# Attention over heads: four row groups of scores per batch, one block of values, and reciprocals written wide and turned

## What is computed

```python
x = rmsnorm(layernorm(hidden), norm_w)
q = (x @ wq.T).reshape(B, L, NH, HD)
k = (memory @ wk.T).reshape(B, M, NH, HD)
v = (memory @ wv.T).reshape(B, M, NH, HD)
attn = softmax(where(mask, einsum('blhd,bmhd->bhlm', q, k) * scale, -inf))
out = einsum('bhlm,bmhd->blhd', attn, v).reshape(B, L, C) @ wo.T
x = x + tanh(g) * sigmoid(x @ wg.T) * out
```

## Time and profile before

| | |
|---|---|
| median of 3 runs | 1286.46 us (1286.46 to 1287.14) |
| profiled execution, its span | 1286.6 us |
| PE busy | 1210.8 us |
| DVE busy | 676.6 us |
| ACT busy | 578.8 us |
| first scores to last values of the first attention | 34.9 to 419.6 us |

### The profile page before, as it was taken

One profiled execution on the slowest core, in us unless ns is written; L12 is line 12 of the kernel. 1 busy time (PEld: TensorE's weight loads), 2 busy tenths in 40 slices (PEclk: granted clock), 3 DMA queues, 4 the chain that ended last, 5 costly groups with the idle time before them and its releaser, 6 DMA issues. The chain is left out here.

```text
span 1286.6 us, 25693 instructions
## 1 busy us (share of the span) xinstructions
PE 1210.8 (94%) x7835; PEld 1023.1 (80%) x7836; DVE 676.6 (53%) x1411; ACT 578.8 (45%) x1387; POOL 424.5 (33%) x514
## 2 busy tenths in 40 slices
PE   7998999999999879889999998999999999999995
PEld 7877777787787657667777777889999889999995
DVE  6656545545445989944576554642234552424241
ACT  5554445455356768872111112543344453434341
POOL 1102211211213656400015742244434334443443
PEclk9999999999999999989999999999999999999997
DMA  9100000000000122022000413764445766545454
GB/s 334 39 18 20 18 1 20 18 1 18 18 18 2 34 69 65 29 96 85 1 0 2 160 41 130 221 142 85 78 103 117 201 144 146 137 85 136 86 135 71
DMA packets 54335, 100.36 MB, mean 78 GB/s; under 512 B 5094, under 2 KB 21990, under 8 KB 54262
## 3 DMA queue, kind: packets, MB, share of 16 engines
q0 software_dynamic: 15824, 37.76, 15.5%
q1 hardware_dynamic: 38438, 61.65, 14.7%
HBM read 72.91 MB, written 26.48 MB: 77 GB/s over the span
## 5 line engine op out<-in xcount | busy, mean ns | idle before, releaser
L1925 PE MATMUL t_H<-m_W,t_xT 128*128 128x352 f32 x1632 | 281.9, 328 | 7.3 <-DVE m_W L2003 5.7
L1925 PEld LDWEIGHTS t_H<-m_W,t_xT 128*128 128x128 f32 x1632 | 263.3, 189 | 10.1 <-DVE m_W L2003 8.1
L1893 POOL DMA_INDIRECT out_dram<-t_ys,t_sid x68 | 109.5, 1610 | 225.0 <-ACT t_ys L1954 110.6
L1970 ACT ACTIVATE t_sl<-t_H 128x352 f32<-128x352 f32 x68 | 31.6, 465 | 175.6 <-PE t_H L1925 175.6
L759 ACT ACTIVATE pr<-SC,neg 128x128 f32<-128x128 f32 x256 | 90.1, 377 | 38.2 <-DVE neg L973 38.2
L47 PE MATMUL t_Y<-m_W,t_hT 128*128 128x512 f32 (+1 forms) x207 | 88.1, 426 | 4.9 <-issue 3.0
L2048 DVE TENSOR_TENSOR t_hT<-t_TH,t_hT 128x384 fp32r<-128x384 f32 x68 | 37.8, 556 | 101.8 <-ACT t_hT L1991 100.6
L2024 DVE TENSOR_TENSOR t_h<-t_H,t_sl 128x352 f32<-128x352 f32 x68 | 35.6, 523 | 104.8 <-ACT t_sl L1970 104.8
L1954 ACT ACTIVATE t_ys<-t_Y,t_wcol 128x512 f32<-128x512 f32 x69 | 47.4, 687 | 95.3 <-PE t_Y L49 95.3
L49 PE MATMUL t_Y<-m_W,t_hT 128*128 128x512 f32 (+1 forms) x207 | 82.5, 398 | 0.0
L48 PE MATMUL t_Y<-m_W,t_hT 128*128 128x512 f32 (+1 forms) x207 | 82.2, 397 | 0.0
(11 more groups left out here) (508 smaller groups left out, 3216.8 us busy)
## 6 DMA issues: line engine op xcount, KB each, us to landing
m_raw<-in_L_ffn_w_dram SPq DMA_DIRECT2D x28, 704.0 KB, 5.3
m_raw<-in_L_ffn_w_dram SPq DMA_DIRECT2D x14, 512.0 KB, 6.8
CT<-in_ctx_dram SPq DMA_DIRECT2D x8, 512.0 KB, 3.7
X<-in_x_dram SPq DMA_DIRECT2D x4, 1024.0 KB, 13.4
rows_d<-rows_first SPq DMA_DIRECT2D x16, 256.0 KB, 2.0
out_dram<-X SPq DMA_DIRECT2D x3, 1024.0 KB, 4.3
m_raw<-in_L_ffn_w_dram SPq DMA_DIRECT2D x14, 192.0 KB, 6.7
CT<-in_ctx_dram SPq DMA_DIRECT2D x8, 256.0 KB, 2.7
```

Source lines behind the costliest of these rows:

```text
L1893: pool.indirect_dma_start(out=m["out_rows"][:, :], out_offset=bass.IndirectOffsetOnAxis(ap=sid[:, b:b + 1], axis=0), in_=ys[:, b, :], in_o ...
L1925: x_ = pe.matmul(bk[b % 2][:, 0:I], xT[:, b % 2, jx, k, :], W13[:, jw, k, j, :], start=k == 0 and jx == jw, stop=k == KC - 1 and jx == 1)
```

## The change

- The scores of a whole batch are one step `S`: four mask matmuls and 16 score matmuls, in four row groups and four banks SC, one bank for each row group. `sm` and `pT` now count heads by row group, and `pT` has four buffers.
- The values of a batch are one step `pv` in a bank of M instead of two in O.
- `rc` writes the reciprocals at once over 128x512, each 32 times, into `o`; `bc` turns `o` with four transposes through T, and ACT copies it back to `o`; the product (formerly `on`) is DVE's part of `pv`.
- `gs` has one buffer instead of two, `mrow` two rows instead of four with `mk` one batch ahead.
- The plan of all four groups is written anew: `pv`, `oT` and `oP` of a batch stand behind the next batch's `S`.

The diff, cut; the removed lines of the plan are in the kernel above.

```diff
         mcol = sb("mcol", [P, NB])
-        mrow = sb("mrow", [P, GB, S], BF16)
...
-        gs = sb("gs", [P, 2, D])
+        gs = sb("gs", [P, D])
...
-        pT = sb("pT", [P, 2, HQ, S])
+        pT = sb("pT", [P, HQ, HQ, S])
...
-        T, M, SC = bank("T", 2), bank("M", 2), bank("SC", 2)
-        O, REC = bank("O", 1)[0], bank("REC", 1)[0]
+        T, M, SC = bank("T", 2), bank("M", 2), bank("SC", HQ)
...
                 break
             plan += steps(
-                f"Sa.0 xT.2 Sb.0 sm.0 sm.1 v.0 st.-2 st.-1 cT.2 ra.-1 xT.3 {d[0]} g.0 rb.-1 pT.0 cT.3 q.1.0 rd.-1 Sa.1 pT.1 Sb.1 "
...
+                f"S.0 pv.-1 sm.0 v.0 oT.-1 xT.2 xT.3 sm.1 oP.-1 pT.0 mk.1 {d[0]} g.0 pT.1 sm.2 q.1.0 st.-2 st.-1 cT.2 sm.3 ra.-1 q.1.1 "
+                f"cT.3 rb.-1 {d[1]} pT.2 q.1.2 rd.-1 {d[2]} pT.3 rc.0 q.1.3 u.-2 sf.-4 sf.-3 uT.-2 u.-1 bc.0 fm.-2 "
+                f"S.1 pv.0 sm.4 v.1 oT.0 uT.-1 {d[3]} sm.5 oP.0 pT.4 mk.2 {d[4]} g.1 pT.5 sm.6 fm.-1 k.1.0 sm.7 k.1.1 nm.4 nm.5 pT.6 sf.-2 {d[5]} k.1.2 "
+                f"pT.7 rc.1 k.1.3 xT.4 sf.-1 bc.1 "
+                f"S.2 pv.1 sm.8 v.2 oT.1 xT.5 cT.4 sm.9 oP.1 pT.8 mk.3 {d[6]} g.2 pT.9 sm.10 q.2.0 cT.5 st.0 sm.11 q.2.1 {d[7]} pT.10 q.2.2 "
+                f"nm.6 nm.7 pT.11 rc.2 q.2.3 bc.2 "
+                f"S.3 pv.2 sm.12 v.3 oT.2 {d[8]} sm.13 oP.2 {d[9]} pT.12 st.1 mk.4 ra.0 g.3 pT.13 sm.14 rb.0 k.2.0 sm.15 rd.0 k.2.1 pT.14 u.0 k.2.2 "
+                f"pT.15 rc.3 uT.0 u.1 k.2.3 bc.3 fm.0 uT.1 fm.1 ", g)
         plan += steps(
-            "Sa.0 xT.2 Sb.0 sm.0 sm.1 v.0 st.-2 st.-1 cT.2 ra.-1 xT.3 g.0 rb.-1 pT.0 cT.3 cx.0 cx.1 q.1.0 rd.-1 Sa.1 pT.1 Sb.1 "
...
+            "S.0 pv.-1 sm.0 v.0 oT.-1 xT.2 xT.3 sm.1 oP.-1 pT.0 mk.1 g.0 pT.1 sm.2 q.1.0 st.-2 st.-1 cT.2 sm.3 ra.-1 q.1.1 "
+            "cT.3 cx.0 cx.1 rb.-1 pT.2 q.1.2 rd.-1 pT.3 rc.0 q.1.3 u.-2 sf.-4 sf.-3 uT.-2 u.-1 bc.0 fm.-2 "
+            "S.1 pv.0 sm.4 v.1 oT.0 uT.-1 sm.5 oP.0 pT.4 mk.2 g.1 pT.5 sm.6 fm.-1 k.1.0 sm.7 k.1.1 pT.6 sf.-2 k.1.2 "
+            "pT.7 rc.1 k.1.3 cx.2 cx.3 sf.-1 bc.1 "
+            "S.2 pv.1 sm.8 v.2 oT.1 sm.9 oP.1 pT.8 mk.3 ta.0 tb.0 pT.9 sm.10 g.2 tc.0 sm.11 pT.10 an.0 qh.0 ks.0 st.0 "
+            "pT.11 rc.2 bc.2 "
+            "S.3 pv.2 sm.12 v.3 oT.2 sm.13 oP.2 pT.12 st.1 ra.0 g.3 pT.13 sm.14 rb.0 sm.15 an.1 qh.1 ks.1 pT.14 rd.0 u.0 aS.0.0 "
+            "pT.15 rc.3 aT.0 bc.3 pv.3 oT.3 aS.0.1 ag.0.0 aT.1 aS.0.2 ag.0.1 "
             "oP.3 uT.0 u.1 fm.0 ", NG - 1)
...
-        SPLIT, T_KINDS = ("xT", "cT", "aT", "rT"), ("xT", "cT", "aT", "rT", "pT", "uT", "ft")
-        BY_ACT, BY_DVE = ("q", "k", "g", "fg"), ("v", "oP", "fm", "aO")
+        SPLIT, T_KINDS = ("xT", "cT", "aT", "rT"), ("xT", "cT", "aT", "rT", "pT", "bc", "uT", "ft")
+        BY_ACT, BY_DVE = ("q", "k", "g", "fg"), ("v", "pv", "oP", "fm", "aO")
...
+                    elif kind == "bc":
+                        for j in range(KC):
+                            i = pe.transpose(bk[:, j * P:(j + 1) * P],
+                                             o[:, j * P:(j + 1) * P], identF[:, :])
                     else:
...
+                    elif kind == "pv":
+                        for j in range(KC):
+                            for r in range(HQ):
+                                i = pe.matmul(bk[r * HD:(r + 1) * HD, j * S:(j + 1) * S], va[:, j * HQ + r, :],
+                                              pT[:, r, j, :], start=True, stop=True)
                     elif kind == "fg":
                         i = pe.matmul(bk[:, 0:P], c["onesF"][:, :], dg[:, :], start=True, stop=True)
                     else:
...
+                        elif kind == "pv":
+                            pe.wait_ge(t_hi, at(T_KINDS, ("pT", HQ * t + HQ - 1)))
+                            pe.wait_ge(m_dve, at(BY_DVE, ("v", t)))
...
-                        cols = slice(b % 2 * S, b % 2 * S + S)
-                        if not late:
...
-                            wait(pe, p_exp, 2 * t)
-                            if half == 0:
-                                pe.wait_ge(mrow_ready, b + 1)
-                                pe.wait_ge(m_act, max(at(BY_ACT, (n, b // 2, KC - 1)) for n in "qk"))
-                            for e, bk in enumerate(SC):
-                                pe.matmul(bk[:, :].rearrange("p (j m) -> p j m", j=HQ), c["onesB"][e * HD:e * HD + 1, :],
-                                          mrow[e * HD:e * HD + 1, b % GB:b % GB + 1, :].to_broadcast([1, HQ, S]),
-                                          start=True, stop=False)
-                        else:
-                            pe.wait_ge(s_half, 2 * t + 2)
-                        for jj in range(2):
-                            for e, bk in enumerate(SC):
-                                r, slot = (2 * late + e) * HD, 2 * late + jj
-                                i = pe.matmul(bk[:, slot * S:(slot + 1) * S], qT[r:r + HD, b // 2 % 2, 2 * half + jj, cols],
-                                              kT[r:r + HD, b // 2 % 2, 2 * half + jj, cols], start=False, stop=slot == HQ - 1)
-                                if jj:
-                                    i.then_inc(s_fill if late else s_half, 1)
-                    elif kind == "pv":
-                        b, half = t // 2, t % 2
-                        pe.wait_ge(t_hi, at(T_KINDS, ("pT", 2 * t + 1)))
-                        if half == 0:
-                            pe.wait_ge(m_dve, at(BY_DVE, ("v", b)))
-                            wait(pe, o_norm, 2 * b)
-                        for jj in range(2):
-                            j = 2 * half + jj
-                            for r in range(HQ):
-                                i = pe.matmul(O[r * HD:(r + 1) * HD, j * S:(j + 1) * S], va[:, j * HQ + r, :],
-                                              pT[:, r % 2, r // 2 * 2 + jj, :], start=True, stop=True)
-                        i.then_inc(pv, 1)
-                    elif kind == "bc":
-                        pe.wait_ge(o_norm, 2 * t + 1)
-                        wait(pe, r_out, t)
+                    elif kind == "S":
+                        cols = slice(t % 2 * S, t % 2 * S + S)
+                        if t == 0:
...
+                        wait(pe, p_exp, HQ * t)
+                        pe.wait_ge(mrow_ready, t + 1)
+                        pe.wait_ge(m_act, max(at(BY_ACT, (n, t // 2, KC - 1)) for n in "qk"))
+                        for r in range(HQ):
+                            pe.matmul(SC[r][:, :].rearrange("p (j m) -> p j m", j=KC), c["onesB"][r * HD:r * HD + 1, :],
+                                      mrow[r * HD:r * HD + 1, t % 2:t % 2 + 1, :].to_broadcast([1, KC, S]), start=True, stop=False)
                         for j in range(KC):
                             for r in range(HQ):
-                                at_ = col_of(j, r)
-                                i = pe.matmul(REC[r * HD:(r + 1) * HD, j * S:(j + 1) * S],
-                                              rec[:, t % 2, at_:at_ + 1].to_broadcast([P, HD]), identF[:, :],
-                                              start=True, stop=True)
-                        i.then_inc(pv, 1)
+                                i = pe.matmul(SC[r][:, j * S:(j + 1) * S], qT[r * HD:(r + 1) * HD, t // 2 % 2, j, cols],
+                                              kT[r * HD:(r + 1) * HD, t // 2 % 2, j, cols], start=False, stop=j == KC - 1)
+                                if j == KC - 1:
+                                    i.then_inc(s_fill, 1)
...
+                            wait(act, o_lo, t)
+                            act.activation(o[:, :], src, ACT.Copy).then_inc(t_hi, 1)
                         elif kind == "pT":
-                            wait(act, pv, at(PV, ("pv", t // 2 - 1)))
-                            act.activation(pT[:, t % 2, :, :].rearrange("p j m -> p (j m)"), src, ACT.Copy).then_inc(t_hi, 1)
+                            wait(act, m_fill, at(M_KINDS, ("pv", t // HQ - 1)))
+                            act.activation(pT[:, t % HQ, :, :].rearrange("p j m -> p (j m)"), src, ACT.Copy).then_inc(t_hi, 1)
...
                         if kind == "g":
-                            wait(act, m_dve, at(BY_DVE, ("oP", t - 2)))
-                            act.activation(gs[:, t % 2, :], src, ACT.Tanh, scale=0.5).then_inc(m_act, 1)
+                            wait(act, m_dve, at(BY_DVE, ("oP", t - 1)))
+                            act.activation(gs[:, :], src, ACT.Tanh, scale=0.5).then_inc(m_act, 1)
...
                         wait(act, t_fill, at(T_KINDS, ("pT", t - 2)))
-                        wait(act, o_norm, 2 * (t // HQ) - 3)
+                        wait(act, o_norm, t // HQ - 1)
...
                         for slot in range(HQ):
-                            at_ = t % HQ * HQ + slot
-                            i = act.activation(pr[:, t % 2, slot, :], SC[t % 2][:, slot * S:(slot + 1) * S], ACT.Exp, scale=SCALE0,
+                            at_ = slot * HQ + t % HQ
```

(39 more changed lines are left out.)

49 lines of the change are left out of this document (17 added, 32 removed), and 7 rows, old and new, of the table d.

## The result

The changed kernel takes 1332.86 us (median of 4 runs, 1331.27 to 1335.52) where the kernel before takes 1286.8 (4 runs): a ratio of 1.0354, 95% interval 1.0337 to 1.0371. It is 46 us slower; the forecast was 1306, its range ended at 1326. The direction was right, the size was not.

What follows compares the result with a forecast made beforehand. TensorE (PE) was taken as the bound, if other engines answer in time. 1286.6 us plus 13.0 (75 us of first-attention waits, 62 paid by PE's saving) plus 6 for half clock gave about 1306; range 1276 to 1326.

Steps and rivals of the forecast that it cites:

- the half clock: First attention: TensorE at 1.2 GHz after long waits; five drops, 1.2 us of each reaching the end, plus 6 us.
- the total of TensorE's waits: First attention: 75 us of PE waits, from walking the plan's order, engine by engine.
- PE's work: First attention: shorter scores, REC and values take PE's work from 369.4 to 322.7 us, 2.9 us a batch.
- The reciprocal: On DVE, widened from 128x16 to 128x512: 3.2 us each by the slope of two rows, 47 us over 16.
- The kinds of waits: PE idle ahead of oP 0.8 to 1.6 us every batch, uT.-2 5.5, pT.3 1.9, bc.2 1.5.
- the walk: First attention, each operation starting when engine and inputs are ready: 397.7 us against 384.7, plus 13.0; chance 0.57.
- leave 13 us of PE work under a chain scores, exps, reciprocal of 20: Last four batches, without q and k: 93.2 us against 81.1, to the last value matmul.
- of 75 us of waits the saving of PE pays 62: First attention: the balance drawn between PE's waits and its saved work, with plus 13.0 us left.
- The cheap reciprocal: Rival: the wide reciprocal on DVE takes 0.69 us, first attention 368 us, whole 1270, clock mostly unhurt; chance 0.12.
- The dearer reciprocal: Rival: half of the 253 ns is fixed, the wide reciprocal on DVE takes 4.2 us, whole 1320; chance 0.12.
- the in-order walk with too long waits: Rival: a third of the first attention's 75 us of waits is not there, 25 us less, whole 1278; chance 0.10.
- Row groups as pairs: Rival: four row groups run as two pairs, score block 1.74 us, 14 us more, whole 1320; chance 0.05.

Runs made afterwards that it cites:

- The last experiment: The changed kernel, wide reciprocal kept, with only the last four batches of the first attention laid out in the third order: 1306.89 us, ratio 1.0166.
- The filled version: The changed kernel with throwaway matmuls on TensorE in the long waits ahead of bc, uT and three pT: 1318.77 us, ratio 1.0249.
- the third order: The changed kernel with the first attention's plan laid out anew for the new blocks: 1253.69 us with reciprocal narrow (128x16, then copy), 1288.28 us wide.

## Why the prediction was right and wrong

The direction and each kind of wait came as forecast. The steps that failed are two terms of the sum, of nearly the same size: the half clock (6 us put in, 17.6 shown) and the total of TensorE's waits (75 us put in, 86.7 shown). Each was about 12 us too small, and a miss of 12 alone, to about 1318, would lie inside the range of 1276 to 1326. Why each was too small stands below, at "The total of the waits" and "The clock".

- **PE's work.** 322.7 us forecast, 323.9 measured (with the half clock taken out). Right; the four row groups overlap as the column groups do (0.99 us for the score block, 0.87 forecast).
- **The reciprocal.** 3.2 us forecast by the slope of two rows, 3.35 measured. At the prediction's own 14 us for each us, 0.15 us makes 2 us of the miss. The estimate from the Trainium skill, "VectorE: DVE Perf Modes", section "First, the fixed hardware budget" (a repeat count of eight), was 4.4 us; the row speaks against eight cycles for an element. (3353 - 253) / 496 is 6.25 ns, six cycles of the 0.96 GHz that the page gives under "Specifications".
- **The kinds of waits.** Each of them is in the trace: `oP` 0.66 to 1.53 us in 15 batches (0.8 to 1.6 forecast), `pT.3` 1.8 (1.9), `uT.-2` 3.9 and twice 5.29 (5.5), `bc.2` 1.5 (1.5), `bc` of the first group's third batch 7.3 (7). In the second steady group the batches were 31.8, 22.4, 24.3 and 25.9 us, in the first 31.9, 22.4, 24.3 and 27.5, for a forecast of 30.1, 21.7, 23.9 and 25.0. This is the queue order made visible, here at the head of the last group (timeline of DVE, then of PE):

```profile
380.52 3.35 DVE L949 RECIPROCAL o<-some 128x512 f32<-128x512 f32 x1
...
385.57 0.49 DVE L810 TENSOR_SCALAR fu<-fu,fsc 128x512 f32<-128x512 f32 x1
```

```profile
386.20 1.09 PE L497 MATMUL T<-identF,fu 128*128 128x128 f32 x4 [5.29 <-DVE fu L810]
```

- **The total of the waits: mis-sized.** 75 us forecast, 86.7 measured, 11.7 short. By groups the walk had 103.2, 100.7, 100.7 and 93.2 us, without its 6 us for the clock; the stretches are 111.5, 106.1, 104.3 and 106.3: 8.3, 5.4, 3.6 and 13.1 more. These differences hold the half clock too, by half of PE's busy time in the rows above about 5.2, 4.7, 1.3 and 6.6 us. So the largest part of what waits alone add, 6.5 us, is in the last four as well. There the walk gave 20.0 and 21.7 us to the third and fourth batch; their scores start at 412.6 and 436.0 and the last values end at 464, so they took 23.4 and 28. The timeline of PE shows waits that the walk had at most in part:

```profile
427.84 0.63 PE L497 MATMUL T<-identF,pr 128*128 128x128 f32 x4 [1.75 <-ACT pr L733]
431.34 0.89 PE L497 MATMUL T<-identF,pr 128*128 128x128 f32 x4 [2.87 <-ACT pr L733]
434.94 1.09 PE L491 MATMUL T<-identF,o 128*128 128x128 f32 x4 [2.70 <-DVE o L949]
...
452.78 0.63 PE L497 MATMUL T<-identF,pr 128*128 128x128 f32 x4 [2.23 <-ACT pr L733]
...
460.71 1.09 PE L491 MATMUL T<-identF,o 128*128 128x128 f32 x4 [4.05 <-DVE o L949]
```

  The prediction said that these batches "leave 13 us of PE work under a chain scores, exps, reciprocal of 20", as if that were their nature. The last experiment shows that it was the order: the same work in another took 83.0 us. One sentence of the prediction is also wrong in itself: "of 75 us of waits the saving of PE pays 62". The saving is 46.7; the other 15.3 are the idle time that was there before. The sum does not suffer by it.
- **The clock: mis-sized by 11.6 us.** The prediction let 1.2 us of each of five drops reach the end, 6 in all, after one drop of 3.4 us in the earlier trace rows. There were nine stretches at half clock, 51.2 us, five of them 6.8 or 10.2 long, with 17.6 us of extra work. The step that failed is the count and the length, both taken from the one row of before. Beside the waits of 6.7 us (ending at 62.3), 7.3 (118.1) and 5.3 (386.2) the clock was down for 6.8, 10.2 and 6.8 us; beside another wait of 5.3 (281.9) for only 3.4. Waits that the prediction did not count had drops too: two of 1.5 and 1.6 us ahead of 226.8, those of 1.8 and 2.9 us in the last group ahead of 431.6. The filled version shows the cause: 14 us come back.
- **The sum.** Clock 11.6, waits 11.7, work 1.2 less saved: 24.5, which is the 43.5 measured in the stretch less 19 forecast.
- **The rivals.** The cheap reciprocal was to give 1270 at 0.69 us; at 0.68 it gives 1297. So even with the reciprocal's size right, this rival's sum was too low, by 27 us (it had left out the half clock, which that version has too, its granted clock being 0.94 to 0.97), and by the groups again mostly in the first and last (103.4 and 96.0 us against 94 and 85.8; the stretches between took 97.6 and 99.5 against 94.1). The dearer reciprocal fell with its row, the in-order walk with too long waits fell by its sign: they were too short. Row groups as pairs were real as a price, 16.6 us, and not what happened.
- **The Trainium skill**, "TensorEngine Tiling (Array Packing)", section "Performance Considerations", warns that with packed tiles the emptying of PSUM can become the limit. The trace agrees only in that PE is idle more, 86.7 us instead of 15.3: its two largest waits, 28.5 and 16.6 us, end with the reciprocal and the quantiser, which read SBUF. In the third order with a narrow reciprocal the same packing leaves 24.4 us idle.

## What to carry to other kernels

When work is taken from the engine that bounds, first list what was hidden under it. Here 45 us less of TensorE's work gave +46, 0 or -33 us, by the order of the queues and one reciprocal on VectorE alone. A rearrangement that saves small instructions must not widen a reciprocal: take it over the few numbers and spread them with a copy (0.68 us against 3.35). In a walk price the last group, where long projections run out, as its own case, and do not count the half clock once for each long wait: two waits of 5.3 us had 3.4 and 6.8 us of it beside them, and pairs of short waits had it too.
